# Batches sorted by role on the chip in a four-layer sequence model: one role per adapter tile, adapter biases as products with rows of ones, x and out moved batch by batch

## What is computed

```python
# L0, L2: block. x is (32, 64, 512), H = 2048
q = x @ Wq; k = x @ Wk; v = x @ Wv
attn = softmax(q @ k.T * scale)
attn_out = (attn @ v) @ Wp + bp
cms_out = gelu(attn_out @ cW1 + cb1) @ cW2 + cb2
cms_out = cms_out + one_hot(target_codes)[:, None, :]
modifier = gelu(concat([attn_out, cms_out]) @ mW1 + mb1) @ mW2 + mb2
x = clip(x + cms_out + modifier, 0, 1)
# L1, L3: adapter. role is one number per batch (1 or 2 of 3 roles)
h = gelu(x @ W_down[role] + b_down[role])      # 512 -> 256
u = h @ W_up[role] + b_up[role]                # 256 -> 512
y = x + u
x = layernorm(y) * gamma[role] + beta[role]
```

## Time and profile before

| what | value |
| --- | --- |
| time, median of 3 runs | 2171.19 us (2169.8 to 2171.62) |
| the profiled execution's own time | 2169.23 us |
| its span in the trace | 2167.4 us |
| PE busy | 2130.0 us (98%) |
| DVE busy | 1421.1 us (66%) |
| ACT busy | 864.5 us (40%) |
| POOL busy | 363.4 us (17%) |

### The profile page before, as it was taken

How to read it: one execution, slowest core, us unless ns; L and a number is a source line. 1 busy time by engine, 2 the same in 40 slices (tenths; PEclk the granted TensorE clock), 3 DMA queues, 4 the chain that set the end, 5 groups by cost and what they waited for, 6 DMA issues and landing times.

```text
span 2167.4 us, 28421 instructions
## 1 busy us (share of the span) xinstructions
PE 2130.0 (98%) x10112; PEld 1785.5 (82%) x10112; DVE 1421.1 (66%) x2249; ACT 864.5 (40%) x1484; POOL 363.4 (17%) x356
## 2 busy tenths in 40 slices
PE   9999999999999999999999999999999999999996
PEld 7888888888888888888878888888888888888885
DVE  6587775566567777655667778555655777756564
ACT  5454443333354444333345445333334544433331
POOL 0011021210401111221231111211031111121204
PEclk9999999999999999999999999999999999999998
DMA  8111212114421122112730111122262011121135
GB/s 318 72 30 59 78 40 68 68 64 149 109 78 49 49 74 69 44 58 68 241 110 30 59 49 64 59 68 68 93 180 93 30 51 57 68 68 64 49 104 135
DMA packets 46281, 178.05 MB, mean 82 GB/s; under 512 B 5954, under 2 KB 10050, under 8 KB 39234
## 3 DMA queue, kind: packets, MB, share of 16 engines
q1 hardware_dynamic: 46146, 176.25, 25.1%
HBM read 159.45 MB, written 16.78 MB: 81 GB/s over the span
## 4 chain that ended last, share of the span: by engine, by line
PE 63%; DVE 3%; DMA 2%; issue 1%; POOL 1%; SPq 1%; ACT 1%; DVEq 0%; POOLq 0%; ACTq 0%
PE psum L482 59%; DMA rolep<-roles_in 1%; DMA raw_u<-up_in 1%; PE psum L764 1%; PE psum L730 1%; PE psum L556 1%; PE psum L578 1%; DVE wup L1061 0%; SPq L322 0%; SPq L321 0%; POOL yt L465 0%; POOL yt L467 0%; DVE xs L1061 0%; DVE stats L1366 0%; DVE yt L1364 0%
## 5 line engine op out<-in xcount | busy, mean ns | idle before, releaser
L482 PE MATMUL psum<-hs,wd 128*128 128x512 f32 x3072 | 716.8, 389 | 0.0
L482 PEld LDWEIGHTS psum<-hs,wd 128*128 128x128 f32 x3072 | 576.3, 188 | 120.9 <-issue 1.4
L1225 DVE TENSOR_TENSOR acc<-psum,acc 128x512 f32<-128x512 f32 x480 | 311.9, 683 | 111.5 <-PE psum L482 111.3
L482 PE MATMUL psum<-cop,wsm 128*128 128x512 f32 x1416 | 354.7, 389 | 0.0
L482 PE MATMUL psum<-aop,wsm 128*128 128x512 f32 x1320 | 332.9, 389 | 0.0
L482 PEld LDWEIGHTS psum<-cop,wsm 128*128 128x128 f32 x1416 | 265.8, 188 | 55.2
L482 PE MATMUL psum<-aop,wsc 128*128 128x512 f32 x1320 | 310.7, 389 | 0.0
L482 PEld LDWEIGHTS psum<-aop,wsm 128*128 128x128 f32 x1320 | 247.8, 188 | 51.4
L482 PEld LDWEIGHTS psum<-aop,wsc 128*128 128x128 f32 x1320 | 247.5, 188 | 51.4
L941 ACT ACTIVATE hs<-psum,bias 128x512 fp32r<-128x512 f32 x88 | 60.8, 691 | 445.6 <-PE psum L482 445.6
L1061 DVE TENSOR_TENSOR hs<-zt,hs 128x512 fp32r<-128x512 f32 x256 | 180.2, 704 | 85.6 <-ACT zt L942 85.6
(11 more groups left out here) (119 smaller groups left out, 2357.1 us busy)
## 6 DMA issues: line engine op xcount, KB each, us to landing
w1m<-m_in SPq DMA_DIRECT2D x32, 1024.0 KB, 4.9
rolep<-roles_in SPq DMA_DIRECT2D x64, 384.0 KB, 4.7
w1c<-c_in SPq DMA_DIRECT2D x32, 512.0 KB, 3.6
w<-c_in SPq DMA_DIRECT2D x32, 512.0 KB, 3.7
w<-m_in SPq DMA_DIRECT2D x32, 512.0 KB, 3.6
fw<-fused SPq DMA_DIRECT2D x6, 2048.0 KB, 11.1
fused<-fw SPq DMA_DIRECT2D x4, 2048.0 KB, 7.5
raw_u<-up_in SPq DMA_DIRECT2D x4, 1536.0 KB, 8.9
```

Source lines behind the costliest of these rows:

```text
L482: mm = nc.tensor.matmul(out, lhs(a), rhs(b), start=(start and n == 0), stop=(stop and n == total - 1), skip_group_check=reopened)
L1225: nc.vector.tensor_tensor(dst, d_out[o][:, :], dst, ALU.add).then_inc(acc_done, 1)
```

## The change

The batches are put in another order before anything else. `rank_batches` (DVE, 40 small steps, counted in the semaphore `ranked`) works out a permutation `order` of the 32 batches: sorted by role, except that the last batch of a role with an odd number of batches goes to the end. With two roles in 32 batches, every tile then holds one role; only the last tile of the second half may hold two (`general(half, i)`), and it keeps the old form in `xzg` and `hzg`. A tile of one role has 12 down and 6 up products in place of 24 and 12. The bias is added by one further product of each kind, with two rows of ones (`onz`) against the HI and LO rows of the biases (`brow`), so the additions of b_down (L1346) and b_up (L1364) are gone: gelu, the statistics and the normalisation read the PSUM banks.

The x and out transfers follow the order, so they are per batch and their place is read from `order` by SP: 16 x loads per half in place of two, two stores per tile in place of one. The gains of a tile are two transfers of 64x1024 elements. The up weights are loaded earlier and split in three parts, two of them in the last unit. x of a pass is always written to `xmid` and read back from there. The diff, cut to its core:

```diff
@@ sync @@
-            for b in range(NTB):
-                sp.dma_start(x[:, :, b * TB:(b + 1) * TB], x_in[0, b]).then_inc(x_loaded[b], 16)
+            def load_x(half, j):
+                sp.nop(nofuse=True)
+                r = sp.value_load(order[0:1, half * NB + j:half * NB + j + 1], min_val=0, max_val=BATCHES - 1)
+                sp.dma_start(x[:, j, :, :].rearrange("p k t -> p (k t)"),
+                             x_in[bass.ds(r, 1)].rearrange("o p n -> (o p) n")).then_inc(x_loaded[j // (NB // 2)], 16)
+
+            sp.wait_ge(ranked, RANKED)
+            for j in range(NB):
+                load_x(0, j)
...
             for n in range(2 * LAYERS):
                 sp.wait_ge(fused_lo, KC * (n + 1))
                 sp.dma_start(fused[n], fw[:, n % 2, :, :].rearrange("p l n -> p (l n)").bitcast(F32)).then_inc(fuse_stored[n % 2], 16)
...
                 for i in range(TILES):
                     if i < TILES - 2:
                         load_gb(i + 2)
-                    store(i)
-                    if i < TILES - 5:
-                        load_bd(i + 5)
+                    if layer == 1:
+                        store(i)
+                        if half + 1 < HALVES:
...
+                            for j in range(3 * i, min(3 * i + 3, NB)):
+                                load_x(half + 1, j)
@@ tensor, front @@
-                for b in range(2):
+                for b, role in enumerate(r):
                     for k in range(KC):
                         for a, c in PRODUCTS:
...
+                    ones = (first_ones, last_ones)[b] if general(half, i) else all_ones
+                    mm = nc.tensor.matmul(out, ones, brow[:, bass.ds(role * BN, BN)], start=False, stop=(b == len(r) - 1))
                 mm.then_inc(dp_done, 1)
                 if i >= 3:
-                    pe.wait_ge(y_done, e - 2)
+                    pe.wait_ge(yn_done, e - 2)
@@ vector @@
                         down_part(p, u)
                         hidden(p, u, H11)
+                        up_part(p, 0)
+                        up_part(p, 1)
                         make_z12(p, u)
...
                     def row_stats(i):
                         e, s = 8 * p + i, i % 2
-                        dve.wait_ge(gb_loaded[s], params(i))
                         dve.wait_ge(up_done, e + 1)
...
-                        nc.vector.tensor_tensor(rows, u_bank[i % 3][:, :], rolep[s][:, BN:BN + V], ALU.add).then_inc(y_done, 1)
-                        dve.wait_ge(y_done, e + 1)
-                        nc.vector.bn_stats(stats[:, s, :], rows).then_inc(st_done, 1)
+                        nc.vector.bn_stats(stats[:, s, :], u_bank[i % 3][:, :]).then_inc(st_done, 1)
...
-                        nc.vector.tensor_scalar(y[i % 4], y[i % 4], mv[:, s, 0:1], rstd[:, s, :], ALU.subtract, ALU.mult).then_inc(yn_done, 1)
+                        nc.vector.tensor_scalar(y[i % 4], u_bank[i % 3][:, :], mv[:, s, 0:1], rstd[:, s, :], ALU.subtract, ALU.mult).then_inc(yn_done, 1)
```

More of the change, by code:

```diff
@@ L145, in cond_seq_kernel @@
         xc = [xct[:, s, :, :] for s in range(2)]
-        hp = [hpt[:, s, :] for s in range(2)]
+        all_ones, first_ones, last_ones = onz[:, SEQ:3 * SEQ], onz[:, 2 * SEQ:4 * SEQ], onz[:, 0:2 * SEQ]
         hg = [hgt[:, s, :] for s in range(2)]
@@ L266, in w_source, with general, x_chunk, x_tile @@
                     P7: w_block(u, 1, 0), P4: w_block(u, 1, 1), P3: w_block(u, 0, 1)}[i]
+        def general(half, i):
+            return half == HALVES - 1 and i == TILES - 1
+        def x_chunk(k, b):
+            return x[:, b * (NB // 2):(b + 1) * (NB // 2), k, :]
+        def x_tile(i):
+            return x[:, 2 * i:2 * i + 2, :, :].rearrange("p b k t -> p k b t")
         def x_block(k, b):
@@ L372, in one_pass @@
                     if kind_of(u):
-                        o, b = u % NG % KC, u % NG // KC
-                        if u > NG:
-                            sp.wait_ge(xadd_done, NG * p + u - NG)
-                        src = xmid[b, :, o, :] if layer else x_in[half, b, :, o, :]
-                        sp.dma_start(xp[:, :], src).then_inc(xp_loaded, 16)
+                        n = u - NG
+                        if n:
+                            sp.wait_ge(xadd_done, NG * p + n)
+                        sp.dma_start(xp[:, :], xmid[:, n * TB:(n + 1) * TB]).then_inc(xp_loaded, 16)
+                    if u + 1 == UNITS:
+                        sp.wait_ge(prod[P6], STRASSEN * (p + 1))
+                        if p == 0:
+                            sp.wait_ge(rows_stored, 16)
+                        sp.dma_start(brow[:, :].bitcast(F32), brows[2 * layer:2 * layer + 2]).then_inc(brow_loaded, 16)
+                        sp.wait_ge(prod[P2], STRASSEN * (p + 1))
+                        sp.dma_start(raw_u[:, :], up_in[layer]).then_inc(uw_loaded, 16)
+                        sp.wait_ge(prod[P7], STRASSEN * (p + 1))
+                        for i in range(2):
+                            load_gb(i)
                     sp.wait_ge(d_lo, first + u + 1)
@@ L381, in one_pass @@
                 sp.dma_start(raw_d[:, 2 * KC * BN:], down_in[layer, :, 2 * KC * BN:]).then_inc(dw_loaded[1], 16)
-                sp.wait_ge(prod[P3], STRASSEN * (p + 1))
-                load_bd(0)
-                load_gb(0)
-                sp.dma_start(raw_u[:, :], up_in[layer]).then_inc(uw_loaded, 16)
-                for h in (H00, H11, H10, H01):
-                    sp.wait_ge(h_lo[h], first + UNITS)
-                load_bd(1)
-                load_gb(1)
-                sp.wait_ge(dw_lo, ROLES * (p + 1))
-                if layer == 1 and half + 1 < HALVES:
-                    for b in range(NTB):
-                        sp.dma_start(x[:, :, b * TB:(b + 1) * TB], x_in[half + 1, b]).then_inc(x_loaded[b], 16)
-                load_bd(2)
-                load_bd(3)
                 if p + 1 < PASSES:
-                    sp.wait_ge(uw_lo, p + 1)
+                    sp.wait_ge(uw_lo, ROLES * (p + 1))
+                    sp.wait_ge(prod[P3], STRASSEN * (p + 1))
                     nxt = 0 if layer == 0 else 2
@@ L448, in _ @@
                     pool.wait_ge(xs_lo, 2 * KC * p + 1)
+                    if layer:
+                        pool.wait_ge(tb_done, 8 * half + 5)
                     nc.gpsimd.memset(pblk, 0.0).then_inc(p_zeroed, 1)
@@ L711, in tile_roles @@
                 pe.nop(nofuse=True)
-                return [pe.value_load(roles[0:1, bass.ds(half * NB + 2 * i + b, 1)], min_val=0, max_val=ROLES - 1)
-                        for b in range(2)]
+                j = half * NB + 2 * i
+                return [pe.value_load(roles[0:1, j + b:j + b + 1], min_val=0, max_val=ROLES - 1)
+                        for b in range(1 + general(half, i))]
             def front(p, half, i):
@@ L792, in _ @@
                             turn_back(p, half, i - 2)
-                        adapter_up(p, i, r.pop(i))
+                        adapter_up(p, half, i, r.pop(i))
                     if layer == 0:
@@ L1383, in _ @@
                     clip(0)
+                    clip(1)
                     split_x(0)
[L1385 to L1386 removed]
+                    up_part(p, 2)
+                    add(p, layer, last, 1, 0)
                     split_x(1)
[L1388 removed]
+                    add(p, layer, last, 1, 1, 2, 3)
                     clip(2)
                     split_x(2)
[L1391 to L1393 removed]
                     split_h(0)
[L1395 removed]
                     for i in range(TILES):
```

372 lines of the change are left out of this document (247 added, 125 removed).

## The result

| | before | after |
| --- | --- | --- |
| median of the runs | 2170.9 us (4 runs, 2169.8 to 2171.62) | 2183.15 us (4 runs, 2182.85 to 2185.85) |
| ratio | | 1.006, 95% interval 1.0042 to 1.0077 |
| span of the profiled execution | 2167.4 us | 2181.4 us |
| PE busy | 2130.0 us | 2094.2 us |

A forecast was written before the change was run, and what follows sets the result against it. PE was taken to bound the kernel, and after the change DVE's normalisation, which frees the bank, the tile loop. 2169.2 - 45.4 + 9.5 + 6.4 + 14 + 1 = 2154.7; median 2 above: 2157 us, range 2138 to 2177.

The forecast's parts named there:

- The adapter term: Stretches from the first down product to the next pass's first product, all four passes together: -45.4 us.
- (a): Start: SP waits for 40 DVE steps, then makes 16 x loads, so fused stores and attention come later: +9.5 us.
- (b): Last unit of each pass: up-weight parts delay DVE's addition and PE waits 1.6 us, four times: +6.4 us.
- (c): Pass 1: SP's 44 steps delay the last stores, which pass 2's first values wait for: +14 us, bounds 0 to 23.
- (d): Remaining additions: memsets gone from POOL and xmid's extra stores cost 0; PE's clock +1 us, bounds 0 and 4.
- The tile loop after: Adapter's full tiles: PE waits for the normalisation to free the bank; 6.10 us (layer 1) or 6.5, gaining 0.2 each.
- PE as the bound: Rival, chance 0.04: bank free soon enough, PE stays the bound in the adapter; 31 tiles save 2.4 us each, 2097 us.
- SP's step: Rival, chance 0.12: a value load and transfer cost more than 1.3 us; slower from 1.59, 2182 us at 1.7.
- The clock rival: Chance 0.04: PE falls to 1.2 GHz in the tile loop's gaps; 28 tiles x 2.5 = 70 us, 2227 us.

The follow-up runs named there:

- the static loads: Changed kernel with the second half's x loaded in pass 1 by two transfers in given order, without value loads: 2173.6 us, ratio 1.0015.

## Why the prediction was wrong, step by step

The forecast was -14.5 us in the span and the result +14.0, a miss of 28.5. The adapter term is 18.3 of it and (a) 14.3; (b) and (c) came out 3 us better, and the 1 us of (d) for the clock is counted here in the adapter term. Either of the two alone would have left the time inside the range (2175 and 2171 us); both together left it.

- **The tile loop after** was right in kind and failed in size. PE waits for the normalisation, and the halved products save little: shown by the products made twice, which change nothing at 6.39 us per tile. The size was off. The prediction's 6.10 and 6.5 us were 6.39 and 6.84: the normalisation on PSUM took 0.80 (0.64 taken, and 0.69 was the upper bound), and the 7 up products 2.06 (1.85 taken: the product with ones was priced as one more of the others, 0.227).

  The term was -45.4 and came out as -27.1, 18.3 less. Of these, 2.2 are the start value: the prediction took pass 2 before as pass 0, 59.2, and it was 57.0. The other 16.1 are longer stretches. Some 5.5 lie in the tiles from the first full one to the fifth at full clock. The clock, for which (d) took 1 us with 4 as the upper bound, fell in one tile of each pass and cost 1.6 us each time (7.99 for 6.39 in pass 1), 6.4 in all. About 4 are left for the ends of the stretches, where the last back turns of pass 0 wait 2.7 us for POOL and the last tile of pass 3 waits 1.2 us for its gains. A part that the prediction forgot is in pass 2: its last tile holds two roles as well (`general`), and it counted the doubled products in pass 3 alone.
- **(a) SP at the start** is the step that failed in its mechanism. "SP waits for 40 DVE steps (8 take 1.75, so 8 us)" took the steps from rows in which nothing ran beside them. The ranking took 23.5 us, from 21.0 to 44.5, since POOL's three operations of 5 to 6 us each held a DVE step. Without these operations the attention starts at 58.74 against the 59.9 of the prediction. So +9.5 was right for a kernel without POOL's row work and +23.8 is what it was; 14.3 us of the miss are this. (d), which asked only for the memsets that POOL loses, overlooked what POOL gets.
- **(b) The last unit** was right: a wait of 1.40 us in the place named, 1.6 forecast; taking it away gave 5.2 in the total, and the MLP stretches of passes 0, 1 and 3 are 1.4 to 1.7 longer than before.
- **(c) SP in pass 1** was right: steps of (1092.08 - 1083.38)/7 = 1.24 us, and 12.8 us lost in pass 2 where 14 + 1.6 was forecast with its last unit, of which the static loads give back 9.8. Part of it is not waiting but the lower clock between the waits: granted 0.89 over the first 47 us of pass 2.
- **The rivals.** PE as the bound and SP's step are refuted. The clock rival was given 70 us or nothing; it happened in part, in one tile of each pass and in the head of pass 2. The run that fills PE's gaps (down products twice) and the one that shortens them (normalisation first) have a granted clock of 1.00 in the stretches of passes 0 to 2.
- **Before the trace of the change.** The trace of before held the hint that was needed: DVE's four splits of x at the end of pass 1, 0.62 us each elsewhere, take 4.67 us while POOL multiplies and adds.

```profile
1099.53 4.67 DVE L1061 TENSOR_TENSOR xs<-x,xs 128x512 fp32r<-128x512 f32 x4
```

```profile
1099.76 1.60 POOL L465 TENSOR_TENSOR yt<-yt,rolep 128x512 f32<-128x512 f32 x1 [0.72 <-DVE yt L1376]
1101.44 1.61 POOL L467 TENSOR_TENSOR yt<-yt,rolep 128x512 f32<-128x512 f32 x1
```

What stays open: how the 16.1 us divide between clock, step lengths and ends was only read from rows, not separated by a run, and why a single tile falls to the lower clock while its neighbours with the same wait don't isn't known. That POOL's operations held the ranking is shown by the run that removes them and by the one that gives their work to ACT and DVE; by which mechanism is not shown by a run of its own, and a run with the same operations on POOL at another moment wasn't made.

## What to carry to other kernels

When products are taken away from PE, look for the reader that gives back its PSUM bank, and move that before counting the gain: here the removed addition was also the bank's early release. A copy by an idle engine (0.6 us), with the normalisation put ahead of the split, was worth 28 us, 12 more than moving the normalisation alone, and with it the halved down products were worth 37 us in place of 14. Price the products that are added, too: two products with 2 rows cost 1.1 us of a tile. Work put "on an idle engine" is free only if it doesn't hold up the engine that is waited for, as POOL's work held DVE's steps here. A transfer with a value load costs its queue 1.24 us, so a few dozen of them ahead of a store are a wait for whoever needs the store.

## What the runs showed of the hardware

- A DVE step on 128x32 elements or on 128x1, with its operands in SBUF, was held nearly to the end of a POOL operation on SBUF that had begun before it (6.06 beside 6.11, 5.59 beside 6.10, 4.74 beside 5.02 us), while reductions beside the same operations took 0.17 to 0.19. The Trainium skill ("SBUF — State Buffer", Who interferes with whom) says that DVE in its two-port modes, or with two inputs in SBUF, contends with a GpSimd operation that reads SBUF, that the shared ports are an exclusive lock held for the whole instruction by the one that came first, and that a reduction never contends; the rows agree, both for the steps that were held and for the reductions.
- A product of 2 rows with ones lasts 0.38 us over 256 columns and 0.49 over 512, where those of 128 rows have medians of 0.28 and 0.40. In the stream each took 0.5 to 0.6 us of a tile, where a product of 128 rows takes 0.12 and 0.235 (2.87/24 and 2.82/12): it costs more than a full one. Why isn't shown.
- PE's granted clock fell to its lower level, 1.2 GHz, in one tile of each pass, though all full tiles wait 1.8 us (6 up products in 2.80 us in place of 1.63). In the full tiles of the profiled executions with waits of 0.8 us, or with the gaps filled, it stayed at 1.00. The kernel before had a fall in pass 0 too, behind waits of 1.21 and 1.06 us (24 down products in 4.47 us in place of 3.04).
